# Masks for the score maxima of a causal attention layer, moved from matmuls to a VectorE add-and-maximum

## The reference

```python
x = x + attention(layernorm(x))     # 16 heads of 16, rope, causal mask, softmax, output projection
x = x + ffn(layernorm(x))           # every operand fp4 quantised in blocks of 16, SiLU gate, 704 wide
```

```python
att = einsum('bhqd,bhkd->bhqk', q, k) / 4
att = where(tril(ones((t, t))), att, -inf)
att = softmax(att, axis=-1)         # subtracts each query's maximum over its unmasked keys
```

## Time and profile before

| | before |
|---|---|
| median of 3 runs | 1327.4 us (1326.84 to 1329.7) |
| profiled execution, its time | 1327.12 us |
| its span, first to last instruction | 1324.8 us |
| mean granted TensorE clock | 0.974 of full |

### The profile page before, as it was taken

One profiled execution on the slowest core, in us unless ns is written; L12 is line 12 of the kernel. 1 busy time (PEld: TensorE's weight loads), 2 busy tenths in 40 slices (PEclk: granted clock), 3 DMA queues, 4 the chain that ended last, 5 costly groups with the idle time before them and its releaser, 6 DMA issues.

```text
span 1324.8 us, 43878 instructions
## 1 busy us (share of the span) xinstructions
PE 1235.4 (93%) x18934; PEld 712.9 (54%) x18934; DVE 1079.2 (81%) x2434; ACT 773.1 (58%) x1659; POOL 474.7 (36%) x500
## 2 busy tenths in 40 slices
PE   7568899999999999999989899999999999999967
PEld 6445555554555545555546655555555546545445
DVE  5778988978988899899618788899899898994356
ACT  5335566655656446567675456557566585776621
POOL 2956625645231131311106554313213121023346
PEclk9778999999999999999999999999999999999979
DMA  4623322222011000110122312120111100000000
GB/s 107 169 75 103 86 70 58 66 65 58 11 33 35 26 18 11 33 26 11 36 65 59 89 42 58 42 51 10 35 34 35 35 2 19 3 3 17 14 13 16
DMA packets 63901, 57.54 MB, mean 43 GB/s; under 512 B 17359, under 2 KB 57297, under 8 KB 63697
## 3 DMA queue, kind: packets, MB, share of 16 engines
q1 hardware_dynamic: 60680, 53.67, 15.4%
q10 hardware_dynamic: 3028, 1.09, 0.3%
HBM read 37.55 MB, written 16.78 MB: 41 GB/s over the span
## 4 chain that ended last, share of the span: by engine, by line
PE 71%; DVE 16%; POOL 5%; issue 3%; ACT 3%; DMA 2%; SPq 0%; ACTq 0%; POOLq 0%; DVEq 0%
PE bank L911 16%; PE bank L865 14%; PE bank L887 14%; PE bank L923 11%; DVE piece_max L1270 6%; PE bank L1036 5%; PE bank L983 3%; ACT prob L1172 2%; PE bank L1027 2%; PE bank L991 1%; PE bank L918 1%; DVE c_mem L1347 1%; PE bank L998 1%; PE bank L892 1%; DVE c_mem L1337 1%
## 5 line engine op out<-in xcount | busy, mean ns | idle before, releaser
L1172 ACT ACTIVATE prob<-bank 128x512 f32<-128x512 f32 (+3 forms) x1280 | 603.7, 539 | 272.8 <-PE bank L887 150.6
L1270 DVE TENSOR_REDUCE piece_max<-bank 128x1 f32<-128x512 f32 (+14 forms) x1280 | 675.6, 579 | 26.5 <-PE bank L865 13.6
L887 PE MATMUL bank<-q_mem,k_mem 99*32 99x512 bf16 (+15 forms) x5120 | 397.6, 341 | 8.6 <-DVE piece_max L1270 5.2
L865 PE MATMUL bank<-k_mem,q_mem 96*32 96x512 bf16 (+14 forms) x5120 | 388.5, 343 | 6.7 <-DVE piece_max L1270 4.3
L911 PE MATMUL bank<-prob,V 128*32 128x512 f32 (+3 forms) x2560 | 296.2, 534 | 12.2 <-ACT prob L1172 11.7
L1484 POOL TENSOR_TENSOR c_mem<-c_mem 128x256 f32<-128x256 f32 (+2 forms) x74 | 86.4, 1168 | 443.8 <-DVE c_mem L1359 443.8
L887 PEld LDWEIGHTS bank<-q_mem,k_mem 99*32 99x32 bf16 x5120 | 144.6, 96 | 159.1 <-issue 77.3
L865 PEld LDWEIGHTS bank<-k_mem,q_mem 96*32 96x32 bf16 x5120 | 143.4, 97 | 144.7 <-issue 81.8
L892 PE MATMUL bank<-mask_kq,ident_h 128*32 128x128 bf16 (+3 forms) x2048 | 104.8, 201 | 0.0
L911 PEld LDWEIGHTS bank<-prob,V 128*32 128x32 f32 x2560 | 67.8, 110 | 63.6 <-ACT prob L1172 26.3
L870 PE MATMUL bank<-mask_qk,ident_h 128*32 128x32 bf16 x2048 | 93.9, 182 | 0.0
(11 more groups left out here) (173 smaller groups left out, 1390.1 us busy)
## 6 DMA issues: line engine op xcount, KB each, us to landing
parts_dram<-a_mem SPq DMA_DIRECT2D x13, 512.0 KB, 4.0
q_mem<-parts_dram SPq DMA_DIRECT2D x32, 192.0 KB, 3.0
k_mem<-parts_dram SPq DMA_DIRECT2D x32, 192.0 KB, 3.5
q_mem<-parts_dram SPq DMA_DIRECT2D x32, 128.0 KB, 3.0
k_mem<-parts_dram SPq DMA_DIRECT2D x32, 128.0 KB, 3.4
c_mem<-in_L_attn_x SPq DMA_DIRECT2D x30, 128.0 KB, 2.1
out<-c_mem SPq DMA_DIRECT2D x30, 128.0 KB, 1.7
a_mem<-in_L_attn_x SPq DMA_DIRECT2D x13, 256.0 KB, 3.0
```

Source lines behind the costliest of these rows:

```text
L865: m = pe.matmul(b[COLUMNS * h:COLUMNS * (h + 1), of], q_rows(u)[0:TERM_ROWS, h, block * COLUMNS:(block + 1) * COLUMNS], k_rows(k0 // CHUNK ...
L887: mm = pe.matmul(b[k0:k0 + COLUMNS, since:CHUNK], k_rows(j // TPC, g)[:, h, first:first + COLUMNS], q_rows(u)[:, h, since:CHUNK], start=Tr ...
L1172: act.activation(prob[:, n % NP, off:CHUNK], bank_of("st", n)[:, off:CHUNK], ACT.Exp, scale=SCALE).then_inc(drained("st", n)[0], 1)
L1270: r = dve.tensor_reduce(piece_max[:, u % 2, block, slot:slot + 1], bank_of("s1", n)[:, column:column + keys], AX.X, ALU.max)
```

## The change

The masks of the first pass leave TensorE. A new buffer `past_keys` holds, for each of the 4 heads' 32 partitions, 480 zeros followed by the 32 x 32 triangle. For an own part of `keys` columns VectorE adds the last `keys` columns of it to the scores, in place in the bank, and takes the maximum, in one `tensor_tensor_reduce`. Parts of earlier chunks keep the `tensor_reduce`. The cast mask `mask_qk` and its ScalarE copy go; the triangle comes in four DMAs of 4 KB on SP instead of one of 64 KB, and GpSimd clears the zeros at the start. Beside this, rope's first multiplications go in another order, so that the wait for the V projection stands before the third of them instead of the first; the q projection waits only for Wq's transposes, the k projection only for Wk's; and numbers of the planner change, so that the order of the whole kernel is another. The diff, cut to its core:

```diff
-DMA_TURN_NS, DMA_NS, DMA_KB_PER_NS, DIVIDE_NS, BESIDE_NS = 460, 1500, 0.2, 96, 2000
-SOONER_NS = dict(a=0, w=0, xn=10000, s=200, st=0, pv=-100, place=1000, norm=200, c=(0, -2000), tile=1000)
+DMA_TURN_NS, DMA_NS, DMA_KB_PER_NS, DIVIDE_NS, JOIN_NS, BESIDE_NS = 460, 1500, 0.2, 96, 150, 2500
+SOONER_NS = dict(a=0, w=0, xn=10000, s=200, st=0, pv=-1000, place=10000, norm=200, c=(0, -2000), tile=1000)
...
     def do(self, engine, name, ns, after=(), shares=False, divided=False):
         if engine == "pe" and divided != self.divided:
-            ns, self.divided = ns + DIVIDE_NS, divided
+            ns, self.divided = ns + (DIVIDE_NS if divided else JOIN_NS), divided
...
+        if engine == "pool" and self.sharing[0] <= begin < self.sharing[1]:
+            ns += self.sharing[1] - begin
+        if shares:
+            self.sharing = begin, begin + ns
...
-            yield from plan.through(("s1", n), 0.428 * keys + 29 * len(parts) * own,
-                                    "dve", 66 * len(parts) + 1.04 * keys, [("masks",)], [], divided=True)
+            yield from plan.through(("s1", n), 0.428 * keys, "dve", 66 * len(parts) + 1.04 * keys, [],
+                                    [("mask load", 0)], divided=True)
...
-                for n, mask in enumerate((future_keys, past_queries)):
-                    yield when["mask load", n]
-                    sp.dma_start(C[0]["h"][:, n * P:(n + 1) * P], mask[:, :]).then_inc(mask_loaded[n], 16)
+                yield when["mask load", 0]
+                for h in range(GROUP):
+                    sp.dma_start(past_keys[COLUMNS * h:COLUMNS * (h + 1), BANK - COLUMNS:BANK],
+                                 future_keys[0:COLUMNS, 0:COLUMNS]).then_inc(mask_loaded[0], 16)
+                yield when["mask load", 1]
+                sp.dma_start(C[0]["h"][:, 0:P], past_queries[:, :]).then_inc(mask_loaded[1], 16)
...
                         if own:
                             at.wait_ge(k_dealt[g], 16 * len(RUNS) * (k + 1))
-                            at.wait_ge(constants_made, 3)
...
-                                          start=True, stop=not own)
-                        for h in range(GROUP if own else 0):
-                            m = pe.matmul(b[COLUMNS * h:COLUMNS * (h + 1), of.stop - COLUMNS:of.stop],
-                                          ident_h[:, 0:COLUMNS], mask_qk[:, 0:COLUMNS], start=False, stop=True)
+                                          start=True, stop=True)
...
+                        if masked:
+                            at.wait_ge(constants_made, 2)
...
-                for s in range(2):
-                    at.wait_ge(*drained("aw", s))
+                at.wait_ge(*drained("aw", o))
...
-                yield when["mask0",]
-                at.wait_ge(mask_loaded[0], 16)
-                act.activation(mask_qk[:, :], C[0]["h"][:, 0:P], ACT.Copy).then_inc(constants_made, 1)
...
-            at.wait_ge(*filled("v", z))
-            engine.tensor_tensor(to[:, :, 0], qk[:, :, 0], cos, ALU.mult).then_inc(done, 1)
-            yield when["rope1", z]
             if before is not None:
                 at.wait_ge(parts_stored[s], 16 * len(STORES) * a_turn[z])
             engine.tensor_tensor(temp[:, 0], qk[:, :, 1], sin, ALU.mult).then_inc(done, 1)
+            yield when["rope1", z]
+            engine.tensor_tensor(temp[:, 1], qk[:, :, 0], sin, ALU.mult).then_inc(done, 1)
             yield when["rope2", z]
+            at.wait_ge(*filled("v", z))
+            engine.tensor_tensor(to[:, :, 0], qk[:, :, 0], cos, ALU.mult).then_inc(done, 1)
...
-                    for column, block, _, keys, slot, _ in parts:
-                        r = dve.tensor_reduce(piece_max[:, u % 2, block, slot:slot + 1],
-                                              bank_of("s1", n)[:, column:column + keys], AX.X, ALU.max)
+                    for column, block, _, keys, slot, own in parts:
+                        scores, most = bank_of("s1", n)[:, column:column + keys], piece_max[:, u % 2, block, slot:slot + 1]
+                        if own:
+                            at.wait_ge(ones_made, 4)
+                            at.wait_ge(mask_loaded[0], 16 * GROUP)
+                            r = dve.tensor_tensor_reduce(scores, scores, past_keys[:, BANK - keys:BANK], scale=1.0, scalar=LOWEST,
+                                                         op0=ALU.add, op1=ALU.max, accum_out=most)
+                        else:
+                            r = dve.tensor_reduce(most, scores, AX.X, ALU.max)
...
+                pool.memset(past_keys[:, 0:BANK - COLUMNS], 0.0).then_inc(ones_made, 1)
```

More of the change, by code:

```diff
@@ L29 @@
 MASKED = -1.0e30
+LOWEST = -3.0e38
 LN_EPS = 1e-5
@@ L261, in rehearse_attention_weight @@
         yield from plan.load("aq", ("aw load", s), 256)
-        yield from plan.through(("aw", s), 444, "act", 500, [("ident load",), ("aw load", s)])
+        yield from plan.through(("aw", s), 444, "act", 500 if s == 2 else 850, [("ident load",), ("aw load", s)])
     projected = {}
@@ L317, in rehearse_projection @@
         rope, ns = ("dve", 600) if rope_on_vector(z) else ("pool", 1235)
-        for n, after in enumerate(([("drain", "q", z), ("drain", "k", z), ("drain", "table", z), ("v", z)], old("stored", len(STORES) - 1),
-                                   [], [], [("rope1", z)], [("rope3", z)])):
-            yield from plan.step(rope, (f"rope{n}", z), ns, after)
+        for n, after in enumerate(([("drain", "q", z), ("drain", "k", z), ("drain", "table", z)] + old("stored", len(STORES) - 1),
+                                   [], [("v", z)], [], [("rope2", z)], [("rope3", z)])):
+            yield from plan.step(rope, (f"rope{n}", z), ns, after, shares=rope == "dve")
         yield from plan.step("act", ("hi", z), 960, [("rope5", z)])
-        yield from plan.step(rope, ("rest", z), 1130 if rope_on_vector(z) else 2200, [("hi", z)])
+        yield from plan.step(rope, ("rest", z), 1130 if rope_on_vector(z) else 2120, [("hi", z)], shares=rope == "dve")
         plan.start(rehearse_parts(z), pair_sooner(z))
@@ L330, in rehearse_low_part @@
     def rehearse_low_part(z):
-        yield from plan.step("dve", ("lo", z), 1150, [("mid", z)])
+        yield from plan.step("dve", ("lo", z), 1135, [("mid", z)], shares=True)
         for n in range(1, len(STORES)):
@@ L386, in rehearse_probabilities @@
                 room = [("pv", (n - NP) // GROUP)] if n >= NP else []
-                yield from plan.wait([("place", u, 2), ("key ones", c)] + room
+                yield from plan.wait([("place", u, 2), ("key ones", c), ("masks",)] + room
                                      + ([("drain", "st", n - ST_IN_FLIGHT)] if n >= ST_IN_FLIGHT else []))
@@ L411, in rehearse_rounding @@
     def rehearse_rounding(key, width, after):
-        whole, blocks = 64 + 1.04 * width, 90 + 0.5 * width
+        whole = 64 + 1.04 * width
         last = after
-        for n, ns in enumerate((whole, 85, blocks / 2, whole, whole / 2, whole / 2)):
-            yield from plan.step("dve", ("round", n) + key, ns, last, shares=n in (1, 4, 5))
+        for n, ns in enumerate((whole, 90, 62 + 0.39 * width, whole, whole / 2 + 36, whole / 2 + 36)):
+            yield from plan.step("dve", ("round", n) + key, ns, last, shares=n in (1, 3, 4, 5))
             last = [("round", n) + key]
@@ L435, in rehearse_weights @@
             for part in range(weight_parts[n]):
-                yield from plan.through(("fw", n, part), 330, "act", 480, ready + [("ident load",)])
+                yield from plan.through(("fw", n, part), 330, "act", 300 + 190 * (name == "d" and part == 0), ready + [("ident load",)])
                 yield from plan.wait([("drain", "fw", n, part)])
@@ L505, in preln_layer @@
         plan.move("sp", (name, 1), 150)
-    plan.move("sp", ("mask load", 0), 64)
+    plan.move("sp", ("mask load", 0), 32)
     plan.move("sp", ("mask load", 1), 64)
@@ L510, in preln_layer @@
     plan.run(lambda: ("hi", 0) in plan.end)
-    plan.do("act", ("mask0",), 215, [("mask load", 0)])
     plan.do("act", ("masks",), 215, [("mask load", 1)])
@@ L541, in preln_layer @@
         ident_h = sb("ident_h", [P, P], BF16)
[L542 removed]
+        past_keys = sb("past_keys", [P, BANK])
         mask_kq = sb("mask_kq", [P, P], BF16)
```

24 lines of the change are left out of this document (12 added, 12 removed).

## The result

The kernel after has a median of 1307.8 us over 4 runs (1298.3 to 1313.3), against 1327.1: ratio 0.9841, 95% interval 0.9812 to 0.9870. That is 21 us by the ratio, 17 to 25 by its interval, where the forecast's sum had 8.7 us. It lies just inside the range, but the gain is more than twice the forecast one, so its causes have to be looked for anew. The runs of this kernel spread over 15 us where the four of before stay within 3.3. The fastest of them, at 1298.3 us, had the highest mean granted clock, 0.983 of full, and the slowest, at 1313.3 us, the lowest, 0.970.

A forecast was written before the change was run, and what follows sets the result against it. PE was taken to bind almost everywhere, DVE near the start. Masks -12.4, surcharge +4.6, start -0.9 and order 0 gave 8.7 us off the profiled 1327.1: 1318.4, set against the median as 1318.7 us; range 1307 to 1333.

The forecast's parts named there:

- Step 4: Whole kernel's order under the new planner biases: from -6 to +6 us, taken as 0.
- Step 1: Mask matmuls leave PE, 512 parts at 29 ns, 14.8 us in all: -12.4 us on the path.
- Step 2: DVE's combined add and maximum on own parts: 70 ns more each, 35.8 us in all, +4.6 us on the path.
- Step 3: Kernel start: rope's first DVE step begins about 0.9 us sooner, extra mask DMAs cost 0: -0.9 us.
- The order takes the gain back: Rival: PE's idle times grow by some 7 us under the new order: 1326 us, chance 0.12.
- DVE becomes the bound: Rival: from 800 to 1191 us DVE binds if the surcharge passes 164 ns; at 228, 1333 to 1334 us; chance 0.16.
- The maximum costs nothing more: Rival: DVE's new instruction has no surcharge: 1312 to 1314 us, with a good order 1307; chance 0.23.
- The write into the bank halves the rate: Rival: DVE writing to the bank adds 1.04 ns a column on own parts: about 1367 us, chance 0.04.

The follow-up runs named there:

- e3: Kernel after with the masks back on TensorE and the plain maximum on VectorE, order and start as after: 1310.8 us, ratio 0.9867.
- e6: Kernel before, masks on TensorE, with only the three new planner biases (BESIDE_NS 2500, pv -1000, place 10000): 1307.2 us, ratio 0.9851.
- f1: Kernel before with only the planner's place bias at 10000 instead of 1000: 1310.3 us, ratio 0.9862.
- e7: Kernel after with rope's first steps, the wait for V and the projections' weight waits as before, in code and rehearsal: 1318.3 us, ratio 0.9925.
- c2: Control: kernel before with the planner number s at 250 instead of 200: 1344.2 us, ratio 1.0130.
- e5: Kernel after with the three planner biases of before (BESIDE_NS 2000, pv -100, place 1000): 1347.0 us, ratio 1.0151.
- g2: Kernel before with masks moved to VectorE, the three new biases, and the rehearsal's costs told of the move: 1328.4 us, ratio 1.0000.
- e1: Kernel before with the masks moved to VectorE and nothing else, rehearsal and order as before: 1332.8 us, ratio 1.0027.
- f2: Kernel before with only the planner's pv bias at -1000 instead of -100: 1316.4 us, ratio 0.9906.
- f3: Kernel before with only BESIDE_NS at 2500 instead of 2000: 1320.7 us, ratio 0.9944.
- c4: e6 with the planner number s at 250 instead of 200: 1311.8 us, ratio 0.9864.

## Why the prediction was wrong

**Step 4, another order, failed.** I gave it 0, from -6 to +6, "as nothing here gives a sign". It is worth 17.7 us, the edits at the start included (e3), and three biases without the rest 20 (e6). I bounded it by PE's waits and idle time from 150 to 1191 us. There the bound was about right: PE idles 27.4 us in before and 21.4 in e3, 6 us less. But it left out 50 to 150 us, where PE idled 26.6 us in before, 15.3 of them in three waits for GpSimd, and 15.9 in e3, 10.7 less. And it left out the clock, which takes some 7 us less in e3. The waits that I named were not all the right ones either: the wait for the placing was 1.0 us and grew to 6.1 in after, while in f1 the last unit of the first batch is placed 39 us sooner. A sign of the turn of the batch was to be had in the trace: DVE at 59.4 of 100 us from 600 to 700, between stretches at 87% and 82%. I had that row, and used it for PE alone. What in the order brings the idle time there stays open.

**Step 1, the masks leave PE,** was right: -12.4 forecast, -10.8 in before's order, -9.7 in after's. Both fit 29 ns a part with not all of the 14.8 us counting; the 29 ns by themselves were not measured.

**Step 2, DVE's surcharge,** was right in its price and wrong in its share of the path. 47 ns instead of 70, but 14.3 us instead of 4.6 in before's order, 6.2 in after's. I weighed it with DVE's share of the chain, 9.3% and 2.4%. That share is taken before the change; as I read it now, where DVE is busy 92% of a stretch a chain through it lies close behind the one through PE, and added work moves the end over to it. The chains fit this: with the surcharge DVE's share goes from 18% to 26% in before's order, from 7% to 16% in after's, and with the whole move it goes from 14% to 37% under the three biases. The idle 32.1 us of DVE from 800 to 1191 us cover an amount, not a moment: each own part comes with its bank awaited, three pieces later at most (`S_IN_FLIGHT`). And PE had 14.8 us less to do, so DVE's slack was smaller than I read.

**Step 3, the start:** DVE's first rope step begins at 19.13 us in after instead of 19.73, so 0.6 us of my 0.9; e7 could not tell its worth from that of the order.

**The rivals.** "The order takes the gain back" was right that the order can outweigh the rest, and had the wrong sign for this one; c2, e5 and g2 are orders that do what it says. "DVE becomes the bound" comes nearest to what the move does, at under a third of the price that I asked for (47 ns, not 164 to 228): e1 is slower than before. "The maximum costs nothing more" fell with the 47 ns, though its time, 1307 with a good order, is the one that was measured. "The write into the bank halves the rate" fell: 512 columns last 716 ns. The sum came out on the right side by luck: a term I held to be nothing was larger than all others. The move by itself goes the other way than forecast in two orders, +3.6 us in before's and +7 with the three biases, and by -3.5, give or take 5, in after's.

The best kernels here are after (0.9841) and e6 (0.9851), whose intervals overlap. So for this kernel the three numbers are worth the same as the whole change, with the masks where they were.

## What to carry to other kernels

When a change comes with a new schedule, price the schedule first, as the largest unknown, and test it by itself: here it was over 80% of the gain, the edits at the start included, and the change it came with was a loss under the old one. A share of the chain tells what shortening an engine's work gives, not what lengthening another's costs: for that look at its busy share beside the bound and at how few buffers lie between. Before believing a gain from a static order, time a neighbour that differs by a meaningless number; here neighbours lay 1, 2, 7 and 17 us apart.

## What the runs showed that I had not expected

The DVE instruction with an accumulator output is followed by a read of 137 ns (mean of 512), and in the unit shown above the next part starts with that read in all but one case, where it starts 0.04 us later. The surcharge is the custom instruction's own length: 716 ns for 512 columns against 676 for the reduce beside it. TensorE's mean granted clock follows the order too. Its median over a kernel's runs is 0.972 to 0.973 in before, 0.976 in after, 0.978 to 0.979 in e3, f2, f3 and c4, but 0.968, 0.966 and 0.964 in c2, e5 and g2. In c2 (PE, PEld, DVE, ACT, POOL, clock, DMA):

```profile
700.00:800.00 100.00, 91.71 (x1365) 59.86 (x1356) 78.89 (x178) 52.38 (x117) 59.79 (x60) 0.95 0.23 63
```

PE is busy 91.7 of 100 us from 700 on at 0.95, where before has 94.7 at 0.98 and after 98.0 at 1.00. In these rows the stretch with more idle PE time also has the lower clock, so that a poor order is paid for twice. It isn't so for whole kernels: f3 idles as long as before (89.7 and 89.4 us) at a higher clock, and f1 idles 16 us less at the same.
